# A first round laid out anew, and another order of the last nine units, in a two-block graph network kernel

## What is computed

```python
adj_norm = adj / (jnp.sum(adj, axis=-1, keepdims=True) + EPS)
h_neigh = jnp.einsum('bnm,bmf->bnf', adj_norm, x)
h = relu(concat([x, h_neigh]) @ weight + bias)
x1 = layernorm(x + h)
A = (adj != 0)
h = x1
for l in range(5):
    m = h @ weight[l]
    agg = jnp.einsum('bij,bid->bjd', A, m)
    gi, gh = agg @ w_ih.T + b_ih, h @ w_hh.T + b_hh
    r, z = sigmoid(i_r + h_r), sigmoid(i_z + h_z)
    n = tanh(i_n + r * h_n)
    h = (1 - z) * n + z * h
out = layernorm(x1 + h * mask)
```

## Time and profile before

| | us |
|---|---|
| median of three runs | 653.69 (651.63 to 655.01) |
| profiled execution, its own time | 652.51 |
| its span, first to last instruction or transfer | 650.7 |
| PE busy / DVE / ACT / POOL | 614.7 / 506.9 / 412.0 / 376.1 |

### The profile page before, as it was taken

How to read it: one execution, slowest core, us unless ns; L and a number is a source line. 1 busy time by engine, 2 the same in 40 slices (tenths; PEclk the granted TensorE clock), 3 DMA queues, 4 the chain that set the end, 5 groups by cost and what they waited for, 6 DMA issues and landing times.

```text
span 650.7 us, 10112 instructions
## 1 busy us (share of the span) xinstructions
PE 614.7 (94%) x2922; PEld 501.0 (77%) x2922; DVE 506.9 (78%) x1153; ACT 412.0 (63%) x775; POOL 376.1 (58%) x309
## 2 busy tenths in 40 slices
PE   5589999999999999999999999999999999999973
PEld 3467778888888888888888888888888888888852
DVE  2866777788897978888797878889797888967664
ACT  4457475766758576675857667675857667555431
POOL 4426363755657576665757666575756656546252
PEclk9699999999999999999999999999999999999977
DMA  7350311223220312222130222323023130000001
GB/s 236 126 178 22 111 50 71 94 65 97 81 97 18 107 68 81 83 78 97 39 129 25 81 97 64 97 75 102 16 84 93 64 97 0 16 1 16 1 17 33
DMA packets 37423, 47.28 MB, mean 73 GB/s; under 512 B 1408, under 2 KB 18944, under 8 KB 37408
## 3 DMA queue, kind: packets, MB, share of 16 engines
q1 hardware_dynamic: 36368, 46.27, 21.7%
q10 hardware_dynamic: 944, 0.72, 0.3%
q0 software_dynamic: 96, 0.10, 0.2%
HBM read 42.90 MB, written 4.19 MB: 72 GB/s over the span
## 4 chain that ended last, share of the span: by engine, by line
PE 89%; DVE 6%; ACT 2%; DMA 1%; issue 1%; POOLq 0%; SPq 0%; DVEq 0%; ACTq 0%
PE ps_tok L1002 11%; PE ps_tok L1007 11%; PE ps_r L896 5%; PE ps_r L894 5%; PE ps_r L895 5%; PE ps_z L896 5%; PE ps_z L894 5%; PE ps_z L895 5%; PE ps_tok L889 4%; PE ps_b L894 3%; PE ps_b L896 3%; PE ps_b L895 3%; PE ps_b L889 3%; PE ps_hn L896 3%; PE ps_hn L895 3%; PE ps_hn L894 3%
## 5 line engine op out<-in xcount | busy, mean ns | idle before, releaser
L481 POOL TENSOR_TENSOR h_lo<-h,h_hi 128x512 fp32r<-128x512 f32 x64 | 82.7, 1292 | 106.3 <-ACT h_hi L518 106.3
L491 POOL TENSOR_TENSOR z_h<-z_gate,h 128x512 f32<-128x512 f32 x80 | 109.3, 1366 | 54.0 <-ACT z_gate L641 54.0
L518 ACT ACTIVATE tok_hi<-ps_tok 128x512 fp32r<-128x512 f32 x64 | 38.3, 598 | 104.3 <-PE ps_tok L889 104.3
L875 DVE SCALAR_TENSOR_TENSOR r_hn<-ps_hn,gru_bias,r_gate 128x512 f32<-128x512 f32 x80 | 59.9, 749 | 49.1 <-ACT r_gate L631 48.7
L434 POOL TENSOR_TENSOR adjt_lo<-adjt_in,adjt_hi 128x512 fp32r<-128x512 f32 x64 | 81.8, 1299 | 17.2 <-ACT adjt_hi L518 17.2
L1002 PE MATMUL ps_tok<-edges,tok_hi 128*128 (+1 forms) x320 | 89.8, 403 | 2.0 <-DVE tok_lo L657 2.0
L1007 PE MATMUL ps_tok<-edges,tok_lo 128*128 (+1 forms) x320 | 89.2, 402 | 0.0
L569 ACT ACTIVATE ps_in<-ps_in,gru_bias 128x512 f32<-128x512 f32 x80 | 52.8, 660 | 55.3 <-DVE ps_in L771 55.2
L1002 PEld LDWEIGHTS ps_tok<-edges,tok_hi 128*128 128x128 f32 x320 | 60.6, 191 | 17.0 <-DVE tok_lo L657 2.6
L1007 PEld LDWEIGHTS ps_tok<-edges,tok_lo 128*128 128x128 f32 x320 | 61.2, 191 | 14.9
L657 DVE TENSOR_TENSOR tok_lo<-ps_tok,tok_hi 128x512 fp32r<-128x512 f32 x64 | 44.2, 691 | 34.0 <-ACT tok_hi L518 31.8
(11 more groups left out here) (123 smaller groups left out, 1575.0 us busy)
## 6 DMA issues: line engine op xcount, KB each, us to landing
adjt_in<-in_adj_t_dram SPq DMA_DIRECT2D x16, 1024.0 KB, 5.2
adj_in<-in_adj_dram SPq DMA_DIRECT2D x16, 1024.0 KB, 5.6
xt_in<-in_x_t_dram SPq DMA_DIRECT2D x16, 256.0 KB, 2.6
x_in<-in_x_dram SPq DMA_DIRECT2D x16, 256.0 KB, 2.8
out_dram<-y_out SPq DMA_DIRECT2D x16, 256.0 KB, 2.3
wl_t<-in_wl_t_dram ACTq DMA_DIRECT2D x1, 320.0 KB, 6.1
wih_t<-in_w_ih_t_dram ACTq DMA_DIRECT2D x1, 192.0 KB, 3.1
whh_t<-in_w_hh_t_dram ACTq DMA_DIRECT2D x1, 192.0 KB, 8.5
```

What stands on the lines that cost most here:

```text
L481: nc.gpsimd.tensor_tensor(h_lo[made][:], h[made][:], raw(h_hi[made][:]), ALU.subtract).then_inc(s_h_lo, 1)
L491: nc.gpsimd.tensor_tensor(z_h[:], z_gate[:], h[layer][:], ALU.mult).then_inc(s_zh, 1)
L518: return nc.scalar.activation(dst, src, ACT.Copy)
L875: nc.vector.scalar_tensor_tensor(out=r_hn[:], in0=ps_hn[:], scalar=bhh_cols[:, 2:3], in1=r_gate[:], op0=ALU.add, op1=ALU.mult).then_inc(s_ ...
```

## The change

**The first round** (all that window -1 did) becomes a function `first()` on each engine.
- SyncE loads `w0` first, then `xt`, then batch 0's transposed adjacency in four pieces and its adjacency in four, each with its own semaphore, then the weights (formerly on ScalarE's queue), x and `whh`. Batch 1's two adjacencies get buffers of their own (`second_adjt`, `second_adj`) and are issued behind `xt` of batch 1, without waiting for batch 0's to be read.
- TensorE turns a block of zeros 16 times before its first product. The five weight products stand behind the turned neighbour sums.
- VectorE makes batch 0's four `adjt_lo`, and `tok_lo`; GpSimd makes `xt_lo` of batch 1 and `whh_lo`, then `rstd1`. ScalarE makes `w0_hi` and `whh_hi`. The low parts of the weight products stand around `norm1`, and not ahead of `mean_parts`.
- `x1` is split and turned by chunks of 128 columns as it is made; `h_hi[0]` and `h_lo[0]` are made straight from PSUM.

**The last nine units** run in the order 15.0, 14.2, 15.1, 13.4, 15.2, 14.3, 15.3, 14.4, 15.4. Batches 14 and 15 end in consecutive units, so batch 15 uses other tiles for its end (`pre1`, `mv1`, `x1`), and VectorE makes both outputs. The remaining edits (`home`, `until_made`) keep the state tiles of batch 15 apart. The loop's instructions stay.

```diff
-LAST_WINDOWS = (((0, 0), (1, 2), (0, 1), (2, 4), (1, 3)),
-                ((1, 2), (2, 4), (1, 3), None, None),
+LAST_WINDOWS = (((0, 0), (1, 2), (0, 1), (2, 4), (0, 2)),
+                ((2, 3), (1, 3), (2, 4), None, None),
                 (None, (2, 4), None, None, None))
...
-        product_bank = (ps_hn, ps_in, ps_tok, ps_r, ps_z)
+        product_bank = (ps_tok, ps_in, ps_hn, ps_r, ps_z)
...
@@ SyncE, ahead of its windows @@
-            load_xt(0)
             sp.dma_start(w0_in[:].rearrange("p (k d) -> p k d", k=2),
                          w0.rearrange("(k p) d -> p k d", p=P)).then_inc(s_w0, 16)
-            load_adjt(0)
-            load_adj(0)
+            load_xt(0)
+            for j in range(C):
+                sp.dma_start(adjt_in[:, j, :], adjt[0][j * P:(j + 1) * P, :]).then_inc(s_first_adjt[j], 16)
+            for c in range(C):
+                sp.dma_start(adj_in[:, c, :], adj[0][c * P:(c + 1) * P, :]).then_inc(s_first_adj[c], 16)
...
+            sp.dma_start(wih_t[:], wiht).then_inc(s_weights, 16)
+            sp.dma_start(wl_t[:], wlt.rearrange("l p d -> p l d")).then_inc(s_weights, 16)
             load_x(0)
+            sp.dma_start(whh_t[:], whht).then_inc(s_whh_in, 16)
+
+            sp.wait_ge(s_xt_lo, 1)
+            load_xt(1)
+            sp.dma_start(second_adjt[:], adjt[1].rearrange("(c p) m -> p c m", p=P)).then_inc(s_second_adjt, 16)
+            sp.dma_start(second_adj[:], adj[1].rearrange("(c p) m -> p c m", p=P)).then_inc(s_second_adj, 16)
+            sp.wait_ge(s_pre1, 1)
+            load_x(1)
...
@@ GpSimd @@
+            def first():
+                pool.wait_ge(s_xt_hi, 2)
+                nc.gpsimd.tensor_tensor(xt_lo[:], xt_in[:], raw(xt_hi[:]), ALU.subtract).then_inc(s_xt_lo, 1)
+                pool.wait_ge(s_whh, 1)
+                nc.gpsimd.tensor_tensor(whh_lo[:], whh_t[:], raw(whh_hi[:]), ALU.subtract).then_inc(s_whh, 1)
+                pool.wait_ge(s_var1, 1)
+                nc.gpsimd.tensor_tensor(rstd1[:], var1[:], minus_half[:], ALU.pow).then_inc(s_rstd1, 1)
+                pool.wait_ge(s_x1_lo, 1)
+                for j in range(C):
...
@@ ScalarE @@
+            def first():
+                act.wait_ge(s_w0, 16)
+                evacuate(w0_hi[:], w0_in[:]).then_inc(s_w0, 1)
+                act.wait_ge(s_xt_in, 16)
+                evacuate(xt_hi[:], xt_in[:]).then_inc(s_xt_hi, 1)
+                for half in range(2):
+                    for j in (2 * half, 2 * half + 1):
+                        act.wait_ge(s_first_adjt[j], 16)
+                        evacuate(adjt_hi[:, j, :], adjt_in[:, j, :]).then_inc(s_adjt_hi, 1)
+                    y_hi_of(half, half + 1)
...
+                act.wait_ge(s_second_adjt, 16)
+                for j in (0, 1):
+                    evacuate(adjt_hi[:, j, :], second_adjt[:, j, :]).then_inc(s_adjt_hi, 1)
+                y_hi_of(0, 3)
+                for c in range(C):
+                    act.wait_ge(s_x1, c + 1)
+                    last = evacuate(tok_hi[:, c * P:(c + 1) * P], x1[:, c, :])
+                last.then_inc(s_x1_hi, 1)
+                act.wait_ge(s_x1t, 1)
+                evacuate(h_hi[0][:], ps_b[2][:]).then_inc(s_h0_hi, 1)
...
+                act.wait_ge(s_h0_lo, 1)
+                evacuate(h[0][:], ps_b[2][:]).then_inc(s_h0, 1)
...
@@ VectorE, first() @@
+                for half in range(2):
+                    for j in (2 * half, 2 * half + 1):
+                        dve.wait_ge(s_adjt_hi, j + 1)
+                        low_part(adjt_lo[:, j, :], adjt_in[:, j, :], adjt_hi[:, j, :]).then_inc(s_adjt_lo, 1)
...
+                moments1(w)
+                product_low((0, 1))
+                norm1(w)
+                product_low((2,))
+                dve.wait_ge(s_x1_hi, 1)
+                low_part(tok_lo[:], x1[:].rearrange("p c d -> p (c d)"), tok_hi[:]).then_inc(s_x1_lo, 1)
+                product_low((3, 4))
+                dve.wait_ge(s_h0_hi, 1)
+                low_part(h_lo[0][:], ps_b[2][:], h_hi[0][:]).then_inc(s_h0_lo, 1)
...
@@ VectorE, last windows @@
+                        if w.first == B + 2:
+                            v = Window(B, B + 1)
+                            dve.wait_ge(s_stored, v.freed(16))
+                            normed(v, y_out, pre2, mv2, rstd2)
+                            normed(w, x1, pre1, mv1, rstd1)
...
@@ TensorE @@
+            def first():
+                pe.wait_ge(s_const, 3)
+                for _ in range(WARM):
+                    turn(ps_z[:, 0:P], zeros[:])
+                pe.wait_ge(s_w0, 18)
+                pe.wait_ge(s_xt_lo, 1)
+                own_products(0)
+                own_products(1)
+                pe.wait_ge(s_first_y, 1)
+                neighbour_sums((0, 1), 0)
+                pe.wait_ge(s_first_y, 2)
+                neighbour_sums((2, 3), 0).then_inc(s_nsum, 1)
+                pe.wait_ge(s_own, 1)
+                sums_by_tokens(1)
+                pe.wait_ge(s_weights, 2 * 16)
+                for l in range(LAYERS):
...
+                for c in range(C):
+                    pe.wait_ge(s_x1, c + 1)
+                    last = turn(ps_b[2][:, c * P:(c + 1) * P], x1[:, c, :])
...
-                    if slot == 1 and w.idles():
-                        last_state()
...
                     if unit:
                         state_products(slot)
+                    if slot == 1 and w.idles():
+                        last_state()
```

437 lines of the change are left out of this document (240 added, 197 removed).

## The result

The changed kernel takes **636.93 us** (median of four runs, 636.37 to 637.19) against 654.06 (651.63 to 655.01) for the kernel before on the same chip: a ratio of 0.974, 95% interval 0.971 to 0.977. The profiled execution took 637.05 us with a span of 635.2. The forecast was 637.7, with a range of 634.5 to 642.5. The span shrank by 15.5 us; the sum of the prediction had 16.0.

The account below looks back on a forecast made before the run. TensorE was busy throughout the loop, so only the two ends counted: 652.51 us less 9.4 (first round) and 6.6 (last nine units) is 636.5; 1.2 added for the median gives 637.7 us, range 634.5 to 642.5.

Parts of the forecast that it names:

- First round: Start of the kernel, up to unit 0.1's aggregation: gain 10.1 us, less 0.7 for handoffs between engines, 9.4 us.
- Transfers: New queue laid on the old transfer curve: transposed pieces at 4.8 to 7.5 us, batch 1's xt at 14.3.
- signs: Right: first aggregation 19 to 21 us, unit 15.4 6.5 us after 14.4. Wrong: first pieces 1 us or more apart.
- Turns of zeros: TensorE before its first products: end between 3.5 and 5.1 us, full clock for the products, worth 0.3 us at most.
- Up to the turned sums: Batch 0's products, neighbour sums and turns: sums end at 10.7 us, turns at 12.1, variance at 16.0.
- Up to x1: Normalisation in the first round: GpSimd's power waits for whh_lo, ends at 18.35 us; norm1 at 19.5, aggregation at 19.85.
- Chunks: tok_hi on ScalarE in four chunks: 0.23 us each taken, bounds 0.16 to 0.38.
- Window 0: From unit 0.0's aggregation on: state products at 22.4 us against 32.47, gate products at 24.95 against 35.12.
- the late transfers: Rival, chance 0.17: the first round's queue delivers late, batch 1's adjacency parts 3 to 4.3 us later, 640.6 to 642 us.
- End: Last nine units: unit 15.4 follows 14.4 by 6.47 us, gates at 629.8 instead of 636.53; gain 6.6 us, bounds 5.8 to 7.3.
- The clock: Rival, chance 0.18: TensorE's clock falls between the weight products and window 0, gates 1.0 us later, 638.7 us.
- the other two: Rivals, 0.03 each: queue transfers don't overlap, 667.7 us; or something unseen holds batch 0's chain, about 651.

Follow-up runs that it names:

- e11: Changed kernel with bias and gru_bias transfers on SyncE's queue behind the eight pieces, mask_cols issued after batch 0's power: 635.97 us, ratio 0.974.
- e9: The changed kernel run once more, unedited, as a control: 638.31 us, ratio 0.977.
- e1: Changed kernel with the order, buffers and norm code of the last nine units as before the change: 644.39 us, ratio 0.987.
- e2: Changed kernel without the 16 turns of zeros: 638.40 us, ratio 0.978.
- e3: Changed kernel with GpSimd's three small transfers issued only after the second piece of the transposed adjacency has landed: 637.88 us, ratio 0.977.
- e10: Changed kernel with 20 turns of zeros instead of 16 and 14 more behind the own products: 637.52 us, ratio 0.977.
- e4: Changed kernel with batch 0's two adjacencies as one 1 MB transfer each instead of four of 256 KB: 639.64 us, ratio 0.979.
- e8: Changed kernel with batch 1's xt ahead of layer weights, power ahead of whh_lo, tok_hi ahead of batch 1's adjt_hi, two small transfers later: 641.87 us.
- e12: Changed kernel with small transfers moved off GpSimd's early queue, 7 fillers, batch 1's xt ahead of layer weights, and ScalarE's order changed: 637.71 us, ratio 0.976.
- e5: Changed kernel with the four low parts of batch 0's transposed adjacency on GpSimd instead of VectorE: 637.74 us, ratio 0.978.
- e6: Changed kernel without own buffers for batch 1's adjacencies, which go into batch 0's: 638.19 us, ratio 0.978.
- e7: Changed kernel with x1's high part made in one 512-column instruction instead of four chunks: 639.38 us, ratio 0.980.

## Why the prediction was right

**First round, 9.4 predicted, 9.26 measured** (43.17 to 33.91). Several instants inside it were off, and the path was the one named, for a reason not seen in full.

- *Transfers.* First xt 4.1 (measured 4.46), pieces 4.8 and 5.6 (5.59 and 7.96), batch 1's xt 14.3 (15.33). The first two pieces are 2.4 us apart, and "1 us or more apart" was one of my signs of being wrong. The second piece is the step that failed: I laid the new queue on the old curve and left out that the bias transfer on GpSimd's queue would now lie beside small pieces. e11 shows its share: 1.9 us of the second piece, 0.9 of batch 1's xt.
- *Turns of zeros.* They end at 5.2, by the slow end of what was laid out (0.21 us each), and the products run at 0.12 us each. e9 has the same turns and products at 0.21. So the full clock there was not bought by the turns for certain, and it was not on the path either. The Trainium skill (TensorE: Matmul & The Clock Gate, Part 1, "What's actually happening") has activity release the throttle, and the point at which it does vary from run to run. The trace agrees with the second part above all: the same turns had done it by 5.96 us in the changed kernel and not by 9.0 in e9.
- *Up to the turned sums.* Sums done at 12.9 (10.7 predicted), variance done at 18.3 (16.0): the 2.2 us of the second piece, carried on.
- *Up to x1.* This is why the 2 us cost only one. The power was forecast to wait for `whh_lo`, from batch 1's xt on: 14.9 plus 3.4 is 18.35 for its end. It ended at 19.4, 1.05 later, as the xt was. Over seven profiles (changed, e1, e2, e3, e9, e10, e11) the mark follows the time at which that xt is read within 0.05 us, from 14.45 to 16.72, e9 less its low clock. The variance itself ended only 0.03 us after `whh_lo` in these. Where GpSimd was idle (e4 to e8, e12) that instruction took 0.17 us, beside `whh_lo` 0.3 to 0.9. So it looked as if both had come together. They nearly had: in e4, e5 and e6, where the sums gate, the mark comes 27.3 us after the sums' end, which for the changed kernel would be 40.2, 0.2 before the 40.39 measured. The slack of 1.25 us that the prediction had between the two (18.35 less 17.1) had been eaten up, and by these figures a second piece 0.3 us later still would have cost time.
- *Chunks.* 0.27 us each (0.23 taken), 0.3 us gained (e7).
- *Window 0.* State products at 23.3 (22.4), gates 25.6 (24.95), unit 0.1 at 33.9 (33.1 by the gain of 10.1, and 33.8 with the 0.7 held back for handoffs). That reserve went to the late xt. It was not made for that, and that the two are of a size is luck. Two slips in the working are small: the 32.47 and 35.12 are chain times, 0.2 us behind the starts in the timeline (32.27 and 34.96), and the "4.3 later" of the late transfers comes out at 3.8 when the same bytes are laid at 253 GB/s from 6 us on, which takes the rival's 642 to 641.5.

**End, 6.6 predicted, 6.25 measured.** The unit's pitch is the term that was mis-sized: 6.71 and not 6.47. At three turns of h (587.3, 600.4 and 614.0 us) TensorE has waited about 0.2 us for that h, and the row reads 0.63 us instead of 0.60; before, one turn in this stretch did (609.3). Two more such waits are 0.4 us and more: the lead over the kernel before falls from 9.15 to 8.90 us at the first of them, and the pitch of the last unit has the other. `agg_lo` follows the h of 14.4 as laid out (620.11 to 620.80), `pre` and the statistics fit behind it, and after the gates the last 14.3 us are as long as before (620.88 to 635.2; 636.4 to 650.7).

**The time, 637.7 forecast, 636.93 measured.** The sum gave 636.5 for a profiled execution, which took 637.05, and added 1.2 because the runs of the kernel before lay that far above their profiled one. The changed kernel's four runs do not (their median is 0.1 below), so this step failed, and it more than made up for the 0.5 us that both ends together gave less. The same kernel a second time (e9) has 638.31. That both are within 0.8 us of the forecast is partly luck; the 15.5 us of span against 16.0 is the firmer agreement. Of the signs, the first aggregation (21.06 for "19 to 21") and the pitch (6.71 for 6.5) are just missed, and `tok_hi` waits 0.25 us for x1.

**The rivals.** The clock (0.18) fell in no row of the changed kernel's first profile, but in e9's, at the own products and at unit 0.1 and not at window 0's aggregation, and it cost 1.4 us where I had 1.0. The median of e9, 638.31, is near this rival's 638.7. The late transfers were right in kind and small in size: 1.0 us at batch 1's xt. The Trainium skill (DMA: Bandwidth & Descriptors, "Measured (HBM→SBUF, 128 partitions, SWDGE, issued from GpSimd)") asks for 1 MiB or more per transfer, from figures for transfers that GpSimd issues; these are issued by SyncE. Here, with eight pieces of a quarter of that on the queue, all transfers moved 206 GB/s from 4 to 6 us, 333 from 6 to 9 and 384 from 9 to 14, against 309, 253 and 373 with the larger ones before, and the last piece of the transposed adjacency landed 0.13 us after the whole one of e4. The measurement decides against the rule for this case, but for the stretch from 4 to 6 us, where the small transfers lie beside the pieces. Nothing speaks for the other two.

## What to carry to other kernels

Where a kernel has a long steady loop, take one instant just behind its first round as a mark: it resolves a tenth of a microsecond where the runs scatter by several. A stall shown on the path need not be worth its length: ask what else arrives at the same instruction, and from which transfer. Read a group of instructions one by one before calling them all slow: a row of four in 1.79 us was one at 1.02 and three at 0.33 (e8). And an order of transfers is judged by the last reader that gates the path, here batch 1's xt through two low parts on GpSimd, not by the first wait in the timeline.

## What the runs showed of the hardware

- With the small transfers (99 KB in all, or in e8 the 64 KB of the bias alone) on GpSimd's queue beside the pieces, all transfers together move 95 to 195 GB/s between 4.5 and 6.75 us (nine profiles, 129 in e9); without them 324 to 341 (e3, e11, e12). The second piece lands 1.9 us later for it (7.93 in e9, 6.05 in e11). On SyncE's queue behind the pieces two of them cost no such time. Beside whole adjacencies (e4) the same three leave 330 GB/s there, but 247 from 6 to 9 us, where the pieces have 333: with pieces their cost falls early, on the piece that TensorE needs first.
- The clock of one instruction stream differs from execution to execution in the first 40 us (e9), by 1.4 us at one place: the aggregation of unit 0.1 behind a pause of 1.41 us, which is as long in the changed kernel's profile, where the clock held.
- Some of VectorE's operations that only read SBUF are held while an instruction of GpSimd runs, and end with it: the 4-column variance takes 0.30 to 0.89 us instead of 0.17 and ends 0.03 us behind `whh_lo` (17.43 and 17.40 in e11), one of the `edges` takes 1.50 instead of 0.41 and ends 0.3 behind it (e5), the first quarter of x1's normalisation 1.02 instead of 0.33, 0.1 behind (e8). Operations that read PSUM kept their times (`y_lo` 0.42 in e5, `wc_lo` 0.55 in the changed kernel). The Trainium skill (Trainium Architecture — The Big Picture, "What this means for kernel authors") calls the port pair that the two engines share an exclusive lock, not a split of the bandwidth; these ends behind GpSimd's agree.
